# A half tile in layer 0, channel sums in one operation, and one wait fewer, in a recommender's interaction kernel

## The reference

```python
x0 = xk = inputs                                   # (B, 39, 16)
for idx, (W, b) in enumerate(params):              # W: (39, fields of xk, 128)
    z = jnp.einsum('bhd,bkd,hks->bsd', x0, xk, W) + b[None, :, None]
    z = jax.nn.relu(z)
    if idx != n_layers - 1:
        half = z.shape[1] // 2
        xk = z[:, :half, :]
        direct.append(z[:, half:, :])
    else:
        direct.append(z)
logit = jnp.sum(jnp.concatenate(direct, axis=1), axis=-1)
...
h = jnp.concatenate([z, dense_ctx], axis=1)        # z: the logits, (2048, 256)
h = jnp.maximum(h @ W_top1 + b_top1, 0.0)
h = jnp.maximum(h @ W_top2 + b_top2, 0.0)
y = h @ W_top3
```

## Time and profile before

| | |
|---|---|
| median of three runs | 2491.62 us |
| profiled execution | 2490.02 us |
| its span, first to last instruction | 2488.2 us |
| mean granted clock of TensorE | 0.996 |
| TensorE busy | 2399.6 us (96%) |
| VectorE busy | 2240.9 us (90%) |
| GpSimd busy | 1679.1 us (67%) |
| ScalarE busy | 1058.4 us (43%) |

### The profile page before, as it was taken

One profiled execution on the slowest core, in us unless ns is written; L12 is line 12 of the kernel. 1 busy time (PEld: TensorE's weight loads), 2 busy tenths in 40 slices (PEclk: granted clock), 3 DMA queues, 4 the chain that ended last, 5 costly groups with the idle time before them and its releaser, 6 DMA issues. The chain is left out here.

```text
span 2488.2 us, 29429 instructions
## 1 busy us (share of the span) xinstructions
PE 2399.6 (96%) x7702; PEld 1442.7 (58%) x7702; DVE 2240.9 (90%) x1657; ACT 1058.4 (43%) x1053; POOL 1679.1 (67%) x1059
## 2 busy tenths in 40 slices
PE   0899999999999999999999999999999999999989
PEld 0465555665565666556556655656665555665556
DVE  0799998999999999999999999999999998999993
ACT  0244443444444444444444444443444443444445
POOL 7877766767677676777767677776768767544340
PEclk9999999999999999999999999999999999999999
DMA  6888787998778789888779887888988777888730
GB/s 162 203 197 196 193 191 183 208 215 191 190 199 191 196 212 213 189 190 199 191 196 216 207 190 187 201 192 197 215 210 188 192 197 173 210 205 195 182 79 11
DMA packets 172546, 469.79 MB, mean 189 GB/s; under 512 B 28987, under 2 KB 63163, under 8 KB 172245
## 3 DMA queue, kind: packets, MB, share of 16 engines
q1 hardware_dynamic: 148869, 461.35, 76.7%
q0 software_dynamic: 19968, 5.15, 2.2%
q10 hardware_dynamic: 3680, 2.95, 0.5%
HBM read 457.02 MB, written 12.33 MB: 189 GB/s over the span
## 5 line engine op out<-in xcount | busy, mean ns | idle before, releaser
L638 POOL TENSOR_TENSOR low<-prod,high 128x1024 fp32r<-128x1024 f32 x384 | 945.9, 2473 | 553.7 <-ACT high L801 551.2
L914 DVE TENSOR_TENSOR prod<-spread,maps 128x2048 f32<-128x2048 f32 x448 | 1016.7, 2281 | 72.8 <-ACT direct L743 20.9
L801 ACT ACTIVATE high<-prod 128x1024 fp32r<-128x1024 f32 (+1 forms) x576 | 596.2, 1056 | 715.9 <-DVE prod L914 458.4
L616 POOL DMA_INDIRECT landed<-in_tbl,rows_id x585 | 620.6, 1061 | 165.6 <-issue 148.6
L1014 PE MATMUL zacc_a<-prod,w_plain 128*128 128x512 f32 (+1 forms) x1536 | 709.1, 596 | 17.0 <-DVE prod L899 11.1
L1014 PE MATMUL zacc_b<-prod,w_plain 128*128 128x512 f32 (+1 forms) x1536 | 706.2, 594 | 5.9 <-DVE prod L914 5.9
L1014 PEld LDWEIGHTS zacc_a<-prod,w_plain 128*128 128x128 f32 (+1 forms) x1536 | 291.9, 190 | 288.9 <-issue 259.9
L1014 PEld LDWEIGHTS zacc_b<-prod,w_plain 128*128 128x128 f32 (+1 forms) x1536 | 291.2, 190 | 275.0 <-issue 246.8
L899 DVE TENSOR_TENSOR prod<-shifted,x_thrice 117x1024 f32<-117x1024 f32 x224 | 266.7, 1230 | 66.8 <-DMA shifted<-x_periods 53.7
L1049 PE MATMUL zacc_b<-low,w_high 128*128 128x512 f32 x672 | 281.2, 499 | 6.2 <-POOL low L638 6.2
L1049 PE MATMUL zacc_a<-low,w_high 128*128 128x512 f32 x672 | 280.7, 498 | 0.7 <-DVE low L869 0.5
(11 more groups left out here) (103 smaller groups left out, 1618.9 us busy)
## 6 DMA issues: line engine op xcount, KB each, us to landing
spread<-x_periods SPq DMA_DIRECT2D x608, 512.0 KB, 16.5
shifted<-x_periods SPq DMA_DIRECT2D x188, 468.0 KB
x_thrice<-x_periods SPq DMA_DIRECT2D x93, 156.0 KB
shifted<-x_periods SPq DMA_DIRECT2D x64, 156.0 KB
landed<-in_tbl,rows_id POOLq DMA_INDIRECT x585, 4.6
spread<-x_periods SPq DMA_DIRECT2D x32, 256.0 KB, 20.7
x_periods<-x SPq DMA_DIRECT2D x30, 256.0 KB, 2.2
spread<-features SPq DMA_DIRECT2D x4, 512.0 KB, 4.6
```

What stands on the lines that cost most here:

```text
L616: nc.gpsimd.indirect_dma_start(out=landed[:, f, :], out_offset=None, in_=tables[f], in_offset=bass.IndirectOffsetOnAxis(ap=rows[:, f:f + 1 ...
L638: nc.gpsimd.tensor_tensor(low[0:rows, at_, :], prod[0:rows, at_, :], high[0:rows, slot(j, SPLIT, NH), :], ALU.subtract).then_inc(s_lowp, 1)
L801: nc.scalar.activation(high[0:rows, h, :], made(turn, j)[0:rows, :], ACT.Copy).then_inc(s_round, 1)
L914: nc.vector.tensor_tensor(prod[:, at_:at_ + 2, :], spread[:, t:t + 2, :], maps[:, :].unsqueeze(1).to_broadcast([128, 2, COLS]), ALU.mult). ...
```

## The change

Layer 0's 780 pairs are laid out anew. The first four of its tiles get 11 more rows (117 to 128), which hold shifts 19, 18, 20 and 21 of fields 0 to 10; so the last tile, 26, needs only 40 rows, and becomes stacked (64 rows, of which 24 are zero): `PLAN` has V there in place of F. Its first factor comes from a buffer of its own, `x_last`. Its low part is made two tiles behind the product, at place 28, and its two pairs of matmuls stand at place 28 too. The relu of layer 0 on ScalarE is written one place later (30 in place of 29). Since the count of split tiles is now 24, all four slots of `high` are used in turn to the end of a turn, where before the last ones used three.

`channel_sum` becomes one `tensor_reduce` over 1024 columns, with the sum over the 8 dimensions innermost in its read pattern: successive reads are 128 elements apart.

The place of a stacked tile with nothing before it to finish is no place that s_mm counts on its own (`silent`); the next place counts for two. And `product` waits for one semaphore, s_mm, for a slot that a stacked tile held, where it waited for s_lowv as well.

SyncE issues seven more loads in a turn: five of 11 rows (44 KB each: one for x_thrice, four for shifted) and four of 20 rows (80 KB each) where two of 39 rows (156 KB each) were.

```diff
-PLAN = "FVFPPPFPFFDPFDVFFPFV" "FFFFFFF" "FPFFFVPFDPVFDPPDFPFV"
+PLAN = "FVFPPPFPFFDPFDVFFPFV" "FFFFFFV" "FPFFFVPFDPVFDPPDFPFV"
-RELU0_AT, RELU1_AT, RELU2_AT = N1 + N0 - 1 + 3, N1 - 1 + 2, 3
+RELU0_AT, RELU1_AT, RELU2_AT = N1 + N0 - 1 + 4, N1 - 1 + 2, 3
 def rows_of(j):
     if j in SQUARED:
-        return TRIPLE
+        return HALF if j == SQUARED[-1] else ROWS if j - N1 < len(SPARE_SHIFTS) else TRIPLE
+def low_behind(j):
+    return SUB_D if PLAN[j] == "D" or j == SQUARED[-1] else SUB
...
+            def load_last(n, to, second):
+                for i, (shift, first, gap) in enumerate(LAST_GAPS):
+                    rows = period(n, first + (shift if second else 0), 2 * gap).rearrange("(b t) c -> t b c", b=2)
+                    sp.dma_start(to[2 * LAST_RUN * i:2 * LAST_RUN * (i + 1), :], rows[0:LAST_RUN, :, :]
+                                 ).then_inc(s_shifted[N0 - 1], 16)
...
+                if u < len(SPARE_SHIFTS):
+                    sp.dma_start(shifted[TRIPLE:ROWS, u % RING0, :], period(n, SPARE_SHIFTS[u], SPARE)
                                  ).then_inc(s_shifted[u], 16)
...
+                sp.dma_start(x_thrice[TRIPLE:ROWS, :], period(n, 0, SPARE)).then_inc(s_thrice, 16)
                 for u in range(RING0):
                     load_shifted(n, u)
+                load_last(n, x_last, False)
...
-                for was in held:
-                    if stacked(was[1]):
-                        dve.wait_ge(*low_done(*was))
-                held = [was for was in held if not stacked(was[1])]
...
-                    nc.vector.tensor_tensor(to, shifted[0:rows, u % RING0, :], x_thrice[0:rows, :],
+                    nc.vector.tensor_tensor(to, shifted[0:rows, u % RING0, :], (x_last if u == N0 - 1 else x_thrice)[0:rows, :],
                                             ALU.mult).then_inc(s_square, 1)
...
-                if step == 0:
-                    dve.wait_ge(ready, turn.count(1, 1))
-                    nc.vector.tensor_tensor(src[:, 0:COLS // 2], src[:, 0:COLS // 2], src[:, COLS // 2:COLS], ALU.add
-                                            ).then_inc(s_half, 1)
...
+                dve.wait_ge(ready, turn.count(1, 1))
+                if not turn.odd and (not turn.fixed or turn.number() > 0):
+                    dve.wait_ge(s_feat, turn.count(1, 0))
+                nc.vector.tensor_reduce(sums[:, which, turn.odd, :], src[:, :].rearrange("p (d b) -> p b d", b=ROWS), AX.X,
+                                        ALU.add).then_inc(done, 1)
...
+            def silent(j):
+                return j < TILES and stacked(j) and PLAN[j - LATE] not in SPLIT
...
-                    done.then_inc(s_mm, 1)
+                    if not silent(j):
+                        done.then_inc(s_mm, 2 if silent(j + 1) else 1)
```

More of the change, by code:

```diff
@@ L43 @@
 TRIPLE = FIELDS * PER0
+SPARE = ROWS - TRIPLE
+SPARE_SHIFTS = (19, 18, 20, 21)
+LAST_RUN, LAST_GAPS = 10, ((19, 11, 20), (18, 11, 21))
+LAST_ROWS = 4 * LAST_RUN
 PERIODS = 2
@@ L85, in rows_of, with loads_of, last_pairs @@
     if j in SQUARED:
-        return TRIPLE
+        return HALF if j == SQUARED[-1] else ROWS if j - N1 < len(SPARE_SHIFTS) else TRIPLE
     t = j if j in PAIRED else j - N1 - N0
     return HALF * min(2, FIELDS - 2 * t)
-def shifts_of(u):
-    return min(PER0, SHIFTS - PER0 * u)
+def loads_of(u):
+    return 4 if u == N0 - 1 else 2 if u < len(SPARE_SHIFTS) else 1
+def last_pairs():
+    taken = {min((r, (r + e) % FIELDS), ((r + e) % FIELDS, r)) for r in range(SPARE) for e in SPARE_SHIFTS}
+    for n, (shift, first, gap) in enumerate(LAST_GAPS):
+        for t in range(LAST_RUN):
+            for b in range(2):
+                f = first + gap * b + t
+                g = (f + shift) % FIELDS
+                once = f < FIELDS and min((f, g), (g, f)) not in taken
+                yield 2 * LAST_RUN * n + 2 * t + b, f % FIELDS, g, once
 def stacked(j):
@@ L121 @@
 PARTED0 = N0 - PLAIN0
+def low_behind(j):
+    return SUB_D if PLAN[j] == "D" or j == SQUARED[-1] else SUB
+assert all(i + low_behind(i) <= j + low_behind(j) for i in range(TILES) for j in range(i + 1, TILES)
+           if PLAN[i] in ON_DVE and PLAN[j] in ON_DVE)
 def weight_slot(j):
@@ L462, in load_thrice0 @@
         def load_thrice0(engine, part):
+            if part == 0:
+                engine.dma_start(x_thrice[TRIPLE:ROWS, :], chunk0(0, SPARE)).then_inc(s_thrice, 16)
             for s in range(PER0):
@@ L469, in load_shifted0 @@
         def load_shifted0(engine, u, part):
+            if part == 1:
+                engine.dma_start(shifted[TRIPLE:ROWS, u, :], chunk0(SPARE_SHIFTS[u], SPARE)).then_inc(s_shifted[u], 16)
             for lo, hi in runs_of(PER0 * u, part):
@@ L918, in product, with channel_sum @@
                 nc.vector.tensor_tensor(to, spread[0:rows, t, :], maps[0:rows, :], ALU.mult).then_inc(s_prod, 1)
[L920 removed]
+            def channel_sum(turn, which):
                 src, ready, done = ((direct01, s_z1, s_sum01), (direct2, s_z2, s_sum2))[which]
[L923 to L937 removed]
+                dve.wait_ge(ready, turn.count(1, 1))
[3 more added lines that the diff above has]
+                                        ALU.add).then_inc(done, 1)
             def feature(turn, which):
@@ L950, in emit @@
                     product(turn, j)
-                for kind, behind in (("V", SUB), ("D", SUB_D)):
+                for behind in range(SUB, 0, -1):
                     then, i = (turn, j - behind) if j >= behind else (last, j - behind + TILES)
-                    if PLAN[i] == kind and has(then, i):
+                    if PLAN[i] in ON_DVE and low_behind(i) == behind and has(then, i):
                         low_part(then, i)
-                if turn.real() and 0 <= j - SUM01_AT < 3:
-                    channel_sum(turn, 0, j - SUM01_AT)
+                if turn.real() and j == SUM01_AT:
+                    channel_sum(turn, 0)
                 if turn.real() and turn.odd and j == SUM01_AT + 3:
```

76 lines of the change are left out of this document (39 added, 37 removed).

## The result

The changed kernel took 2596.54 us, the median of four runs (2589.27 to 2598.89); the kernel before took 2490.98 on the same chip. The ratio is 1.042 (95% interval 1.0403 to 1.0436): 4.2% slower, where 0.7% faster was forecast and 2511 us was the upper end of the range. The profiled execution took 2589.27 us, its span 2587.3, at a mean granted clock of 0.988 where before it was 0.996.

The account below looks back on a forecast made before the run. TensorE bounds the kernel at 73.07 us a turn; afterwards VectorE's 72.45 sets it, 0.62 less, 19.2 us over 31 turns. 2490.0 - 19.2 + 1 = 2471.8, with the median 1.6 above the profiled execution: 2473 us, range 2463 to 2511.

Parts of the forecast that it names:

- What bounds the kernel now: Steady part: TensorE sets the pace at 73.07 us a turn; VectorE alone would need 71.66.
- TensorE's part: Tile 26 stacked instead of F gains 0.79 us a turn, bringing TensorE's turn from 72.82 to 72.03 us.
- VectorE's part: VectorE's turn: 1.25 us for tile 26's low part, less 2.72 for old sums, plus two reductions: 72.45 us.
- r: Price of one strided 1024-column reduction on VectorE, taken as 1.13 us from bounds of 1.13 and 2.2.
- Rival A: The strided reduction is slow and VectorE becomes the bound from r = 1.44; 2507 us at 1.67; chance 0.30.
- Where the two meet: At tile 29, VectorE's pair 29/30 is ready at T + 9.3 + r and TensorE wants it at T + 10.4.
- T: The end of tile 19's matmuls on TensorE, from which the prediction counted its times in a turn.
- The sum: TensorE's turn 72.28 us with stray waits, VectorE's 72.45; the latter taken, 0.62 us less than 73.07.
- rival B: VectorE's waits for TensorE and ScalarE (1.41 us a turn) do not shrink; no change, 2492 us; chance 0.15.
- Loads: Seven more issues and 0.23 MB more a turn through SyncE's queue and the DMA engines, costed at nothing.
- rival C: Larger, more numerous loads lengthen VectorE's `shifted` wait; if its 1.55 us a turn double, 2521 us; chance 0.05.
- The start: Layer 0 of turn 0 ends 0.5 us later, and 1 us with a load more in front.

Follow-up runs that it names:

- e3: The kernel before with only `channel_sum` changed to one reduction; ratio 1.002 to the kernel before.
- e13: The changed kernel with channel sums at places 28 and 12 and reductions reading in order (sums of other elements); ratio 0.9992 to the kernel before.
- e14: The kernel before with two reductions reading in order (sums of other elements) at places 28 and 12, without the half tile; ratio 0.9985.
- e7: The changed kernel with tile 26 as an F tile of 64 rows again, all else as changed; ratio 1.0055 to the kernel before.
- e1: The changed kernel with its first channel sum one place later, at 28 in place of 27; ratio 1.0149 to the kernel before.
- e6: The changed kernel, first channel sum at place 28, both reductions reading in order (sums of other elements); ratio 1.0000 to the kernel before.
- e9: The changed kernel with channel sums at places 28 and 12 in place of 27 and 14; ratio 1.0092 to the kernel before.

## Why the prediction was wrong

**What bounds the kernel now**: right. TensorE set the pace with VectorE 1.2 us behind it; e3 used that room up at a cost of 0.2%.

**TensorE's part**: the two pairs of tile 26 are 0.47 us apart as said, and 128 rows cost no more than 117 (0.43 us from start to start). The 0.79 us of matmuls are saved. But even with VectorE relieved (e13 against e14) a turn is only 0.2 us shorter, and the first turns eat that up: "that alone is worth 25 us" took for granted that all that follows TensorE's saving can come as much earlier.

**VectorE's part, "The low part of tile 26 is new: ... 1.25 us"**: this is the step that failed most. The operation takes 2.81 us, because it starts while GpSimd works on tile 28. In the steady part the records of this form are 45.5 us above 1.22, 1.62 us in each of its 28.1 turns. The 1.25 us that the prediction had and these 1.62 make 89 us in 31 turns, the 3.6% between the changed kernel and e7. The price was read from tile 19, where no subtraction of GpSimd's stood beside it; a duration was carried to another neighbourhood. The trace of before held the hint, in the third step of the sum, which the prediction read only as a mean of 495 ns:

```profile
1230.91 2.04 DVE L936 TENSOR_TENSOR sums<-direct 128x128 f32<-128x128 f32 x1
```
```profile
1230.40 2.38 POOL L638 TENSOR_TENSOR low<-prod,high 128x1024 fp32r<-128x1024 f32 x1
```

A step of about 0.28 us took 2.04 here and ended 0.17 us behind GpSimd. Of its 64 records 31 are longer than 0.4 us, so the 2.72 us that the prediction credits for the two sums held some of this stall already. The Trainium skill's "SBUF — State Buffer" (section SBUF: two separate sides) says it outright: a VectorE operation with two SBUF inputs and a GpSimd operation that reads SBUF share a port pair under an exclusive lock, whichever starts first has it for the whole instruction, and the other is blocked. The traces agree. In the 18 of them, 1271 VectorE operations with both sources in SBUF start while GpSimd subtracts (0.02 us or more behind its start, 0.15 or more ahead of its end). All but three end 0.12 to 0.15 us less than their usual length behind GpSimd's end. Two of the three start 0.07 us behind GpSimd and are not held, and there GpSimd's record is 3.5 us instead of 2.4; the third is the one of e7 that stands through three subtractions. Of 7648 with a source in PSUM that start so, none is more than 0.03 us longer than usual, and of 100 reductions none more than 0.04. The prediction did not draw on the page.

**The reduction**: r = 1.13 was taken of bounds 1.13 and 2.2; it is 1.87 (1948 ns less 0.08). "Every VectorE row goes by its column count alone" was true of rows without a stride. Rival A had the mechanism and its break-even, and with the half tile nearly its size: e1 less e6 is 1.5%, 37 us, where the prediction's sum gives 46 (2 x 0.74 us in 31 turns). The Trainium skill's "Vector Engine (DVE) Microarchitecture Reference" (section 5.2 Measured stream behaviour on trn2) gave the estimate of 1.85 us; the trace agrees, 0.71 ns a column over the ordered read (732 ns on 1024) against the page's 0.68. Its figure deserved more weight than the nearest rows, none of which had the access pattern.

**Where the two meet**: the prediction's times, counted from T, can be laid on the turn with T = 1351.51. Pair 27/28 starts at T + 3.6 and ends at T + 5.8, as said. With r at 1.95, the reduction's step from start to start here, pair 29/30 would be ready at T + 11.3; with the low part 1.6 longer it is T + 12.9, and the trace has TensorE starting on it at T + 12.95. The low part, "ready at T + 7.05 + r, wanted at T + 9.5: no wait up to r = 2.4", is ready at T + 10.6. "Meet with nothing to spare" was a warning taken for a fit: what VectorE was late by there, TensorE waited for.

**The sum**: 70.19 + 2 x 1.87 = 73.93 for VectorE; with the stall 75.55; with 0.32 more on the loads 75.87. The remaining waits for TensorE and ScalarE (30.5 us, 1.09 a turn), which the prediction set at nothing, give 77.0, and 0.26 less at "issue" 76.7, where 76.30 was measured. The 0.4 us between them were not traced.

**Waits of VectorE that "do not shrink"** (rival B): they fell from 1.41 to 1.09 us a turn only, with VectorE the slower engine, and rival B's 1.000 is what e6 gave once stall and stride were gone. At pair 27/28 and pair 14/15 it waits for a hand-off whose place in the order is fixed, and is then late at pair 29/30. e9 took those for TensorE away for 0.57%, and others grew.

**Loads** (rival C): VectorE's wait for them is 1.34 us a turn in e3, 1.89 in e7 and 1.87 in the changed kernel, but 1.37 in e1. That they lengthen VectorE's turn where it sets the pace can be; a price of their own is not shown, and the 2 us a turn of the rival are not reached. **The wait fewer**: nothing, as said. **The start**: pair 27/28 of the first layer 0 starts at 86.8 us where it was 85.3, 1.5 us later against 1 forecast.

**Clock**: not in the prediction. At 366 to 370 us TensorE waits 2.06 us for tile 26, and the granted clock of the 4 us from 368 is 0.66, part of it at the lower level, 1.2 GHz. The pairs behind take 1.17 and 1.05 us in place of 0.74 and 0.62:

```profile
368.00:372.00 4.00, 2.54 (x5) 1.61 (x6) 3.97 (x4) 0.70 (x1) 3.24 (x4) 0.66 0.53 132
```
```profile
369.16 1.17 PE L1080 MATMUL zacc_a<-high,w_low 128*128 128x512 f32 x2 [2.06 <-DVE high L913]
370.13 1.05 PE L1083 MATMUL zacc_a<-high,w_high 128*128 128x512 f32 x2
```

Between 205 and 2350 us the changed kernel is at 1.2 GHz in 11 places, 48 us in all, and the kernel before in two, 7 us. If TensorE worked through all of it, that is at most 20 us of the 105 that were lost; how much of it is on top of VectorE's sum above was not separated. The three executions at a mean clock of 0.982 to 0.984 took 7 to 10 us longer than the profiled one at 0.988.

## What to carry to other kernels

Price an operation together with what runs beside it: before adding or moving a VectorE operation with both sources in SBUF, look up what GpSimd does in that stretch, and put there something with an operand in PSUM or a one-source operation. A form whose longest record is several times its usual one (0.28 against 2.04 us here) is worth a look at the other engines' timelines before its mean is used. Relief for the busiest engine is worth only what every hand-off behind it can follow, so compute the lead at each of them, with the upper bound of each unknown price. And a control experiment can bring a cost of its own: e7, meant to isolate the loads, had a 64-row matmul in it that no other version has.

## What the runs showed of the hardware

- A VectorE addition, subtraction or product with both sources in SBUF that starts during GpSimd's tensor_tensor ends its own length, less some 0.14 us, after GpSimd's end: 2.81 for 1.22 us, 2.49 for 0.42, 2.68 for 1.22. It stands through several in a row: 7.92 us beside three (e7, at 254.39). Where VectorE starts first, GpSimd's record is the longer: 3.38 us in place of 2.37 (e1, at 1345.95, with VectorE's at 1345.87).
- The one-source reduction beside GpSimd is not held (2.00 us in e1), and the products with maps in PSUM are not either. Nor does GpSimd's gathering of rows hold VectorE: the low part at 1217.50 in the kernel before takes its 1.22 us beside it.
- A reduction over 1024 columns takes 1216 ns in order and 1948 when each read is 512 bytes on.
- ScalarE, writing 1024 columns with each element 32 bytes on, takes 2130 ns in place of 1111.
- TensorE's f32 matmuls of 512 columns start 0.43 us apart with 117 rows, with 128, and at the step between them. Going from 117 to 64 rows and from 64 to 128 costs 0.2 us each (e7, 22 turns of 22).
